# Third and fourth expert layers: every expert for every token, or runs of the two chosen experts' tokens

## What is computed

```
# L2_ffn: TOP_K = 2, B, S, d, f, E = (4, 512, 128, 256, 8)      gelu,  no biases
# L3_ffn: TOP_K = 2, N_EMBD = 128, D_FF = 512, NUM_EXPERTS = 8  relu,  b1, b2
h = layernorm(x);  logits = h @ wg;  the two best experts of a token, softmax over the two
y = sum over the two of share * (act(h @ W1[e] + b1[e]) @ W2[e] + b2[e]);  x = x + y
```

## Time and profile before

| | us |
|---|---|
| median of 3 runs (1355.45 to 1363.08) | 1357.49 |
| profiled execution, first to last instruction | 1352.5 |
| median less the span | 5.0 |
| third expert layer: its first split activation to its last product | 795.5 to 915.3 |
| from there to the fourth attention's first scores | 915.3 to 942.2 |
| fourth expert layer: its first product to its last | 1147.4 to 1344.9 |
| from there to the end | 7.6 |

### The profile page before, as it was taken

The page is one execution under the profiler, slowest core; times in us unless marked ns, Lnnn a source line. Parts: engine busy times, 40 slices in busy tenths (PEclk is TensorE's granted clock), DMA queues, the critical chain, the costliest instruction groups (busy, mean ns, idle before and its releaser), DMA issues.

```text
span 1352.5 us, 23129 instructions
## 1 busy us (share of the span) xinstructions
PE 1166.6 (86%) x6840; PEld 881.3 (65%) x6840; DVE 947.6 (70%) x2656; ACT 779.7 (58%) x2526; POOL 720.2 (53%) x1208
## 2 busy tenths in 40 slices
PE   4866999948989779279999977996999999889998
PEld 3765888735555468257767655765767766667886
DVE  4564454588887851577667688998666667889887
ACT  2315333348889524068778844453878787656664
POOL 4232666457667444465556644553655575447562
PEclk9876999959999969679999999998999999999999
DMA  2503656480000213201000004320010000032311
GB/s 55 15 20 102 183 180 202 126 151 1 2 1 1 63 50 116 62 1 33 1 1 2 9 1 129 116 77 17 1 48 1 1 17 1 16 95 95 93 33 32
DMA packets 101932, 72.80 MB, mean 54 GB/s; under 512 B 31603, under 2 KB 83371, under 8 KB 101808
## 3 DMA queue, kind: packets, MB, share of 16 engines
q1 hardware_dynamic: 97456, 62.58, 17.8%
q0 software_dynamic: 4352, 8.73, 2.0%
HBM read 61.01 MB, written 10.27 MB: 53 GB/s over the span
## 4 chain that ended last, share of the span: by engine, by line
PE 55%; DVE 21%; issue 8%; ACT 6%; POOL 5%; DMA 4%; SPq 0%; DVEq 0%; ACTq 0%; POOLq 0%
PE ps L2608 8%; PE ps L2610 7%; PE ps L2609 7%; PE ps L2732 5%; PE ps L2746 4%; DVE h_p L2062 3%; PE ps L2760 2%; ACT ex L1398 2%; PE ps L3314 2%; DVE xn_tok L1693 2%; DMA xr<-xr_d,src_i 2%; PE ps L3301 2%; DVE ln_st L1679 2%; PE ps L3305 2%; DVE acc L2081 1%
## 5 line engine op out<-in xcount | busy, mean ns | idle before, releaser
L1082 POOL TENSOR_TENSOR pp<-ex,rc 128x256 f32<-128x256 f32 x384 | 235.5, 613 | 212.4 <-DVE rc L2108 153.6
L1253 ACT ACTIVATE ex<-ps,nmx 128x154 f32<-128x154 f32 x512 | 193.8, 388 | 74.9 <-DVE nmx L2103 73.3
L2103 DVE TENSOR_REDUCE nmx<-ps 128x2 f32<-128x308 f32 x256 | 120.1, 471 | 91.4 <-PE ps L2610 91.2
L2062 DVE TENSOR_TENSOR h_p<-h_f,h_p 128x512 fp32r<-128x512 f32 x192 | 159.9, 868 | 26.4 <-POOL h_p L838 24.0
L838 POOL CAST h_p<-h_f 128x512 fp32r<-128x512 f32 x96 | 80.3, 838 | 118.7 <-ACT h_f L1194 118.4
L2732 PEld LDWEIGHTS ps<-ident,pp 128*128 128x128 f32 x640 | 73.3, 140 | 59.8 <-POOL pp L1083 34.2
L1398 ACT ACTIVATE ex<-ps,nmx 128x154 f32<-128x154 f32 x256 | 97.4, 392 | 22.9 <-DVE nmx L1936 22.5
L1083 POOL TENSOR_TENSOR pp<-ex,rc 128x52 f32<-128x52 f32 x384 | 104.8, 273 | 0.0
L2732 PE MATMUL ps<-ident,pp 128*128 128x128 f32 x640 | 99.1, 279 | 4.5 <-POOL pp L1083 4.5
L1253 ACT ACTIVATION_READ_ACCUMULATOR ex<-ps,nmx 128x1 f32 x512 | 102.8, 201 | 0.0
L2608 PE MATMUL ps<-kp,q_s 128*128 128x308 f32 x256 | 95.7, 374 | 5.4 <-ACT ex L1253 5.4
(11 more groups left out here) (395 smaller groups left out, 3294.5 us busy)
## 6 DMA issues: line engine op xcount, KB each, us to landing
w_r<-in_L_ffn_W SPq DMA_DIRECT2D x69, 256.0 KB, 3.4
wrep<-gate_d SPq DMA_DIRECT2D x32, 256.0 KB, 3.9
xnT<-gate_d SPq DMA_DIRECT2D x32, 256.0 KB, 4.0
w_s<-in_L_ffn_W SPq DMA_DIRECT2D x24, 256.0 KB, 3.2
w_e<-in_L_ffn_W SPq DMA_DIRECT2D x8, 256.0 KB, 4.7
w_s<-in_L_ffn_w SPq DMA_DIRECT2D x16, 128.0 KB, 2.5
xg<-xs_d SPq DMA_DIRECT2D x8, 195.0 KB, 3.8
xs_d<-blank SPq DMA_DIRECT2D x1, 1548.0 KB, 14.9
```

The costliest lines, as they stand in the source:

```text
L1082: pool.tensor_tensor(pp[st % 2][:, m % 4, 2 * j:2 * j + 2, :], w[:, :, 0:P], r.broadcast_to([P, 2, P]), ALU.mult)
L1253: ins = act.activation(ex[:, tt % NEX, j, :], ps[:, tt % 3, j * SK:(j + 1) * SK], ACT.Exp, bias=nmx8[:, tt % 8, j:j + 1], accum_out=sm8[:, ...
L2062: dve.tensor_tensor(lo[:, c, :], h_f[:, (n * k + c) % NHF, :], hi[:, c, :].bitcast(F32), ALU.subtract).then_inc(f_hl, 1)
L2103: dve.tensor_reduce(nmx8[:, tt % 8, :], ps[:, tt % 3, 0:2 * SK].rearrange("p (h s) -> p h s", h=2), AX.X, ALU.max, negate=True).then_inc(n ...
```

## The change

Layers 2 and 3 get the two best experts only, in runs, from **regions**: each expert has 2048 slots of 130 numbers in DRAM (`xq_d`: 128 features, the share, the pair's number). All slots are first filled with zeros and a spare number by SyncE, issued in layer 1 (8.65 MB a layer). Then:

- At the end of the attention VectorE picks the experts (`choose`), ranks the pairs (`ranks`) and computes each pair's slot; GpSimd scatters the normed rows of each batch twice (`scatter_rows`): 32 indirect transfers of 128 rows a layer. From the counts VectorE makes tables of the expert and the first slot of each of the 23 runs.
- `region`, per run k: SyncE reads an expert number and a slot number into registers and issues two weight loads and one contiguous load of 256 rows; TensorE two transposes, nc first products of 128x256, 2 x nc second products of 128x128, in float32 and unsplit; ScalarE copies the columns out and applies the first two activations; VectorE the others (layer 3), the row numbers (`targets`) and the weighing by the share; GpSimd scatters the 256 result rows to the place of their pair in DRAM in two transfers. At the end SyncE reads both halves back, and VectorE adds two addends to `x`.
- On TensorE the second product stands ahead of the later transposes: `hidden(k + 1)`, `down(k)`, `columns(k + 2)`. ScalarE's order is `first_half(k)`, `columns(k + 2)`.
- Splitting, spreading of shares, `finish_of` and the interleaved units are gone. All 13 preparations of the fourth attention stand ahead of its layer norm on VectorE.

```diff
-    DENSE = (2, 3)
-    CNT = (0, 0, 0, 1, 2)
+    REGION = (2, 3)
...
+    SLOTS = B * S
+    EMPTY = E * SLOTS
+    SPARE = 2 * B * S
+    NQ, NX, NY = 4, 8, 6
...
+                def weights(k):
+
+                    u = k % NQ
+                    e = sp.value_load(expert_q[0:1, k:k + 1], min_val=0, max_val=E - 1)
+                    if k >= NQ:
+                        sp.wait_ge(q_yp, run(l, k - NQ) + 1)
+                    sp.dma_start(w1_q[u][:, 0:n * P], t[f["w1"]][bass.ds(e, 1)].rearrange("a p h -> p (a h)")).then_inc(q_w[u], 16)
+                    sp.dma_start(w2_q[u][:, 0:n, :], t[f["w2"]][bass.ds(e, 1)].rearrange("a (c p) d -> p (a c) d", p=P)).then_inc(q_w[u], 16)
...
+                def rows(k):
+
+                    u = k % NX
+                    r = sp.value_load(row_q[0:1, k:k + 1], min_val=0, max_val=EMPTY)
+                    if k >= NX:
+                        sp.wait_ge(*landed(q_out, l, k - NX, 32))
+                    sp.dma_start(xq[u][:, :, :], rows_d[bass.ds(r, RUN), :].rearrange("(p h) c -> p h c", h=HALVES)).then_inc(q_x[u], 16)
...
+                sp.wait_ge(q_xs, 16 * 2 * NT * (l - 1))
+                for k in range(NQ + 2):
+                    rows(k)
+                for k in range(NQ, NRUN):
+                    weights(k)
+                    if k + 2 < NRUN:
+                        rows(k + 2)
...
+                rstd(j, 1)
+                rstd(j, 2)
+                scatter_rows(l, 0, (0, 1))
+                rstd(j, 3)
+                scatter_rows(l, 0, (2, 3))
+                scatter_rows(l, 1, range(TB))
+                scatter_rows(l, 2, range(TB))
+                scatter_rows(l, 3, range(TB))
+                for k in range(NRUN):
+                    pool.wait_ge(q_y, run(l, k) + 1)
+                    for h in range(HALVES):
+                        pool.indirect_dma_start(yq_d[:, :], bass.IndirectOffsetOnAxis(ap=ids_q[:, k, h:h + 1], axis=0),
+                                                yq[k % NY][:, h, :], None).then_inc(q_out[k % NX], 16)
...
+                for k in range(NRUN):
+                    first_half(k)
+                    if k + 2 < NRUN:
+                        columns(k + 2)
...
+                columns(0)
+                columns(1)
+                hidden(0)
+                for k in range(NRUN):
+                    if k + 1 < NRUN:
+                        hidden(k + 1)
+                    down(k)
+                    if k + 2 < NRUN:
+                        columns(k + 2)
```

More of the change, by code:

```diff
@@ L31, in xattn_moe_stack @@
     NEX = 4
-    NHF = 4
     NLN = 9
@@ L625, in raw_weights @@
                         sp.wait_ge(n_wo, 4)
+                    if l == 3 and g < 2:
+                        sp.wait_ge(*full(2, ("prep", g + 2, PREPS - 1)))
+                        sp.wait_ge(n_wo, base(2, 4) + g + 3)
                     if g >= 2:
@@ L1373, in heads1 @@
+                shares(l, 2)
+                tail_xT(l, 3)
+                second_rows(l, 3)
+                shares(l, 3)
+                region(l)
             def heads1():
@@ L1512, in heads1 @@
                     gelus(e)
-            def ffn(l):
-                f = FFN[l]
-                n = f["nc"]
-                for k in range(UNITS, E * B):
-                    hidden(l, k)
             def sorted_runs():
@@ new lines, in rank @@
+            def rank(l, b):
+                pe.wait_ge(q_oh, B * (l - 2) + b + 1)
+                at_ = ps[:, 1, b * TB * E:(b + 1) * TB * E].rearrange("p (n e) -> p n e", e=E)
+                mm(at_, tri[:, :], both[:, tiles(b), :], start=True, stop=False)
+                for k in range(TB - 1):
+                    mm(at_[:, k + 1:TB, :], ones[:, :], both[:, b * TB + k:b * TB + k + 1, :].broadcast_to([P, TB - 1 - k, E]), start=False, stop=False)
+                mm(at_, ones[:, :], total[:, b:b + 1, :].broadcast_to([P, TB, E]), start=False, stop=True).then_inc(q_rk, 1)
@@ L2777, in heads @@
                 s = 2 * l
-                before = [base_ + YD[l] - B for base_ in (min(b + 3, B) for b in range(B))]
                 def preps(first, last):
```

1033 lines of the change are left out of this document (391 added, 642 removed).

## The result

| | us |
|---|---|
| before, median of 16 runs (1355.45 to 1370.65) | 1362.78 |
| changed, median of 16 runs (1343.39 to 1357.53) | 1349.78 |
| ratio, with its 95% interval | 0.9913 (0.9898 to 0.9929) |
| changed, profiled execution, span | 1355.7 |

The change makes the kernel 13 us faster, 0.9%, where 18.7 us were forecast. The profiled execution of the changed kernel is the slowest of its 16 (1357.53 us of device time for a span of 1355.7), while the span of the kernel before, 1352.5, is shorter than that of any of its 16 runs (every run here is 1.7 to 2.2 us longer than its span, and the shortest took 1355.45). So spans of the two profiles must not be subtracted; stretches can be compared one by one.

The account below looks back on a forecast made before the run. TensorE was taken to set the length of the two dense expert layers. Layer 2 -0.9, handover +7.1, layer 3 -35.3 and end +10.4 sum to -18.7 us: span 1333.8, median 1339 us, range 1318 to 1362.

Parts of the forecast that it names:

- The step that failed: Ends of the third and fourth attention: last powers left at their old times, 806.1 and 1163.3 us.
- The chain on GpSimd: Before the first run of layers 2 and 3: 28 scatters after the last power, 1.27 us apart.
- The row of layer 1: Last scatter's issue to first transposes: 5.74 us read from layer 1, 6.5 us with one register load.
- The period of a run: Layer 2: 2.75 us a run, set by SyncE's queue; layer 3: 4.36 us, set by TensorE's chain with the copy's gap.
- The handover: Third expert layer to the fourth attention's first scores: 34 us against 26.9, +7.1 us.
- the end: Behind the kernel's last product: 18.0 us against 7.6, +10.4 us.
- The fill: Filling the regions with 17.3 MB: costed at nothing, with the second attention as its cover.
- The clock in the runs: Layers 2 and 3: clock 1.00 from the third run on; rival of half clock, 1384 us, 7 in 100.
- The second rival: Dearer handovers and loads: 2 us later in each chain, 0.3 us a run more; 1356 us, 17 in 100.
- the sum: Whole kernel: -0.9 + 7.1 - 35.3 + 10.4 = -18.7 us, span 1352.5 to 1333.8.
- From span to median: Whole kernel: median taken 5.0 us above the span, so 1333.8 becomes 1338.8 us.

Follow-up runs that it names:

- e2: Changed kernel with the last batch's residual and statistics ahead of the picking of batch 1, in both layers; ratio 0.9821 to the kernel before.
- e4: Changed kernel plus unread identity products on TensorE where it idled at the attention's end and ahead of the first run; ratio 0.9841 to the kernel before.
- e1: Changed kernel with all eight scatters of batch 0, not four, ahead of the last batch's power on GpSimd; ratio 0.9829 to the kernel before.
- e7: Changed kernel without the second choice's scatters (16 a layer, not 32), so its output lacks that choice; ratio 0.9744 to the kernel before.
- e3: Changed kernel with the transposes of run k + 2 ahead of the second product of run k on TensorE; ratio 0.9744 to the kernel before.
- e6: e3 without the register load of the expert's number in layer 2, so not the chosen expert's weights; ratio 0.9744 to the kernel before.
- e5: Changed kernel with the regions filled twice, measured among the long times; 1392.4 us, ratio 1.0072 to the kernel before at 1383.1.
- e11: Changed kernel without an edit, measured again among the long times; 1396.7 us, ratio 1.0100 to the kernel before at 1383.1.

## Why the prediction was right in its direction and short in its size

- **The step that failed** is "VectorE's new picking and ranking of batches 0 and 1 takes the place of its splits of activations, so I leave these times". The ends of the attentions were put at no change; they took 9.8 and 8.2 us more. Work was compared with work, and neither the place of the new steps in VectorE's order nor what they wait for was. Of the 18.0 us, 13.5 arose ahead of the last projection (3 of them a shift of the mark, the rest by the rows the picking of batch 0 ahead of `oT_s` and a fall of the clock; no run tests it) and 4.4 behind it, where the picking of batch 1 waits 3.7 us for logits and stands ahead of the addition on which the last power depends. e2 shows that the order behind the projection can give back 14 us, more than was lost there; e4 that the clock can give back 6.
- **The chain on GpSimd** (28 scatters, 1.27 us apart) was right to 0.1 us in both layers, e1 shows that it sets the start, and e7 that what lies behind it is 15 us shorter in layer 2 and 12 in layer 3. The row of layer 1 gave 6.5 us from the last issue to the transposes; it was 5.1.
- **The period of a run** came out near the number partly by luck. TensorE's chain was longer than forecast by 0.05 us for the copy and by 0.08 for the first products: 4.49 us in layer 3, not 4.36, and 2.73 in layer 2, not 2.61. In layer 3 this was made up for by an error the other way: the last of the 22 periods, counted whole, holds only the second product (1.7 us), so 96.0 us stand against 95.9. The mechanism, TensorE waiting for the copy, was right (e3). In layer 2 the forecast took SyncE's queue, 2.75 us, as the bound. It was TensorE's chain, 2.73, with SyncE close behind at 2.68; e3 and e6 show SyncE's queue as the bound only once the gap is closed.
- **The handover** (31.9 for 34) and **the end** (19.8 for 18.0) were right within 2.1 us. The end's sum took 9.5 us for the last batch where its row reads 10.5, and besides the last two runs' results come 1.8 us apart and GpSimd needs 2.5 for a run: its last scatter is issued 2.9 us behind the last product, not 1.9.
- **The fill** at nothing: a second fill beside the same attention costs nothing that can be told (e5); the first was not left out in any run.
- **The clock in the runs** stayed at 1.00 in both layers, as the windows from 872.60 and from 1239.90 show, with a gap of 0.52 us in each run. The Trainium skill, "TensorE: Matmul & The Clock Gate", section "A second HAM failure mode: psum-queue depth-cycling", would have had it swing; the trace does not agree. What fell was the clock in front of the runs, where the removed units had kept TensorE at work: a mean of 0.70 and 0.76 where it was 1.00. In e4 products that nobody reads brought it back to 1.00 from 794 to 810.
- The second rival, dearer handovers, had the place partly right (the chain to the first run) and the size wrong: 2 us for each chain, where the last power came 8 to 10 us later and what stood behind it took 1 to 2 us less.
- Put into the sum, +18.0 for the ends and -5.9 for all other lines but the first give -6.6 us between these two profiles without their first 580 us; the medians say -13.0. Single profiles of one kernel differ by as much (the power ahead of the third attention stood between 582.9 and 590.2).
- **From span to median**: the forecast added 5.0 us to the span, the median of three runs less the one profile. Over 16 runs the kernel before has its median 10.3 us above that span. So of the 10.8 us by which 1349.8 lies above the forecast of 1339, 5.3 are the median before, 1362.8 instead of 1357.5, and the rest is the gain of 13.0 instead of 18.7.

## What to carry to other kernels

When work at the end of a stage is exchanged, don't compare the sums of its durations: write down for each new instruction what it waits for and what stands behind it in its engine's order, down to the last one that releases the next chain; here taking an addition out from behind a wait of 3.7 us and what follows it gave 7 us twice, and the steps ahead of the last projection had cost 4 to 6 us twice. The first wait that is found need not be where the time was lost: split the stretch and compare each part with the kernel before. If a chain on one engine sets the start of a stage, fill its gaps with what is ready (e1: one changed line, 10 us). And after a gap is closed ask which queue has the next period: in layer 2 it was SyncE's register loads, then GpSimd's scatters, whose backlog came out again in the handover.

## What was not expected of the hardware

- A scatter of 128 rows of 520 bytes landed 2.4 us after its issue on the median (2.3 at the least), and GpSimd issued one each 1.27 us. The Trainium skill, "DMA: Bandwidth & Descriptors", section "Anatomy of one DMA — SWDGE (gpsimd) path", gives 2.0 us and the bytes by 436 GB/s, an estimate of 2.15 us for these; the trace's median is 0.25 us above it.
- A fill of 17.3 MB in pieces of 4160 bytes a partition ran at 405 GB/s beside an attention (the second fill of e5, 380 to 420) and did not lengthen it against e11.
- The same kernels took 20 us (before) and 50 us (changed) longer in some sets of runs, in the changed kernel's profiles only in stretches whose pace hangs on indirect transfers and register loads (layer 3's runs, with time to spare, stayed at 96.0 us), where steps of SyncE took 0.7 us and more and single waits without a releaser in the profile up to 7.6 us. A gain that rests on many small transfers should be measured in more than one set of runs.
